# The sixth pass's finishing moves into the seventh, two normalisations to the seventh's end, and the gate turns get banks of their own: an attention megakernel on one NeuronCore

## What is computed

```python
xn = _layernorm(x, axis=-1)
s = _L0_attn_ref(xn, ...)              # gated linear recurrence, norm, silu gate, projection
g = _silu(_L0_ffn_ref(xn, ...))        # 8 experts, top 2, gates = softmax of the two logits
x = x + s * g
xn = _layernorm(x, axis=-1)            # "second normalisation" below
s = _L1_attn_ref(xn, ...)              # windowed attention
g = _silu(_L1_ffn_ref(xn, ...))        # ternary feed-forward
x = x + s * g
```

## Time and profile before

| | |
|---|---|
| median of three runs | 3416.82 us (3414.13 to 3417.32) |
| the profiled execution's own time | 3419.85 us |
| its span, first to last instruction | 3418.1 us |
| PE busy | 3286.0 us, 96% |
| DVE busy | 2671.5 us, 78% |
| ACT busy | 1834.8 us, 54% |
| POOL busy | 1272.6 us, 37% |
| mean granted TensorE clock | 0.997 |
| chain that ended last, by engine | PE 71%, DVE 12%, ACT 7%, DMA 4% |
| chain, DMA `g_wide<-gate_rows` alone | 3% |

### The profile page before, as it was taken

How to read it: one execution, slowest core, us unless ns; L and a number is a source line. 1 busy time by engine, 2 the same in 40 slices (tenths; PEclk the granted TensorE clock), 3 DMA queues, 4 the chain that set the end, 5 groups by cost and what they waited for, 6 DMA issues and landing times.

```text
span 3418.1 us, 89893 instructions
## 1 busy us (share of the span) xinstructions
PE 3286.0 (96%) x35134; PEld 2274.5 (67%) x35134; DVE 2671.5 (78%) x6395; ACT 1834.8 (54%) x4088; POOL 1272.6 (37%) x1404
## 2 busy tenths in 40 slices
PE   5999999999999999999999999999999999999998
PEld 3676666766667666676766667666676666766666
DVE  6877878878788777887778777787877878878787
ACT  3364654646546465463655636456364654646546
POOL 4434244242443524425233342423434244242432
PEclk9999999999999999999999999999999999999999
DMA  4002010020100202011020110202002010020110
GB/s 116 22 22 61 23 53 19 25 58 24 52 23 25 54 24 61 15 38 40 24 64 11 54 29 21 63 12 65 18 24 60 24 52 21 22 58 24 52 23 26
DMA packets 110005, 128.56 MB, mean 38 GB/s; under 512 B 23457, under 2 KB 77329, under 8 KB 109585
## 3 DMA queue, kind: packets, MB, share of 16 engines
q1 hardware_dynamic: 104720, 121.13, 13.7%
q10 hardware_dynamic: 4864, 1.69, 0.2%
HBM read 74.01 MB, written 17.30 MB: 27 GB/s over the span
## 4 chain that ended last, share of the span: by engine, by line
PE 71%; DVE 12%; ACT 7%; DMA 4%; issue 3%; POOL 1%; SPq 0%; DVEq 0%; ACTq 0%; POOLq 0%
PE bank L1926 7%; PE bank L1549 5%; PE bank L1945 5%; PE bank L1828 5%; PE bank L1694 4%; PE bank L1863 4%; PE bank L1889 4%; PE bank L1586 3%; DMA g_wide<-gate_rows 3%; PE bank L1711 3%; PE bank L1766 3%; PE bank L1666 3%; PE bank L1651 3%; DVE am L1268 3%; PE bank L1845 2%
## 5 line engine op out<-in xcount | busy, mean ns | idle before, releaser
L901 POOL TENSOR_TENSOR qx<-qx 128x512 f32<-128x512 f32 x256 | 277.5, 1084 | 656.9 <-ACT qx L1139 655.1
L1403 DVE TENSOR_REDUCE row_max<-bank 128x4 f32<-128x384 f32 x512 | 270.8, 550 | 90.6 <-PE bank L1828 90.1
L1268 DVE TENSOR_TENSOR am<-bank,causal 128x512 f32<-128x512 f32 x512 | 327.9, 682 | 17.6 <-PE bank L1666 17.6
L1509 DVE TENSOR_TENSOR sq_lo<-qx,sq_hi 128x512 fp32r<-128x512 f32 x256 | 232.3, 907 | 125.3 <-ACT sq_hi L1127 124.1
L1945 PE MATMUL bank<-pj_t,sq_hi 128*128 128x256 f32 x1024 | 260.3, 288 | 6.2 <-DVE sq_lo L1509 5.5
L1023 ACT ACTIVATE tanh_g<-bank 128x256 f32<-128x256 f32 x128 | 49.2, 384 | 400.8 <-PE bank L1549 400.8
L1549 PE MATMUL bank<-w_vg,xt 128*128 128x512 f32 x512 | 252.3, 615 | 0.0
L1945 PE MATMUL bank<-pj_t,sq_lo 128*128 128x256 f32 x1024 | 251.0, 279 | 0.0
L1586 PE MATMUL bank<-xt,w_down 128*128 128x512 f32 x512 | 237.2, 596 | 0.0
L1139 ACT ACTIVATE qx<-bank,scale_fc 128x512 f32<-128x512 f32 x256 | 177.2, 692 | 98.5 <-PE bank L1931 96.6
L1412 DVE TENSOR_TENSOR am<-bank,row_max 128x384 f32<-128x384 f32 x384 | 212.9, 554 | 9.8
(11 more groups left out here) (278 smaller groups left out, 8523.1 us busy)
## 6 DMA issues: line engine op xcount, KB each, us to landing
g_wide<-gate_rows SPq DMA_DIRECT2D x64, 512.0 KB, 6.1
x<-in_L_attn_x SPq DMA_DIRECT2D x128, 128.0 KB, 2.3
qt<-in_L_attn_x SPq DMA_DIRECT2D x128, 128.0 KB, 2.5
out<-x SPq DMA_DIRECT2D x128, 128.0 KB, 1.7
k<-k SPq DMA_DIRECT2D x96, 128.0 KB, 2.4
xl<-xh SPq DMA_DIRECT2D x48, 128.0 KB, 2.4
xl<-xn SPq DMA_DIRECT2D x48, 128.0 KB, 2.3
xh<-xn SPq DMA_DIRECT2D x48, 128.0 KB, 2.3
```

The lines of the kernel that those rows point to most:

```text
L901: nc.gpsimd.tensor_tensor(sq[:, n % 3, :], relu[:, n % 3, :], relu[:, n % 3, :], ALU.mult)\
L1268: nc.vector.tensor_tensor(am_tiles[:, :, j], bank[3 + j][:].rearrange("p (f e t) -> p f e t", f=2, e=2), causal[:].unsqueeze(1).unsqueeze( ...
L1403: nc.vector.tensor_reduce(row_max[:, j, :], bank[1 + j][:, 0:4 * KW].rearrange("p (h k) -> p h k", k=KW), AX.X, ALU.max, negate=(j == 0)). ...
L1509: nc.vector.tensor_tensor(sq_lo[:, n % 3, :], sq[:, n % 3, :], sq_hi[:, n % 3, :].bitcast(F32), ALU.subtract)\
```

## The change

`first_queries_keys` gets a table of banks in place of 4 + n % 4; only n = 6 changes its bank by it, from 6 to 2. `experts_down` 0 to 3 moves from banks 0, 1, 2, 3 to 2, 3, 7, 6. The gates' transposes keep banks 1 and 0, which now hold nothing of this sequence's head, and no longer wait for two Relus. ACT's two copies of gate rows move ahead of the copies of queries and keys 4 and 5. On DVE the second `finish_chunk` of pass 5 is gone, `finish_chunk(4)` runs in the gap of pass 6, only two of the four `normalise2` stay in that gap, and the other two run after `project_gated(5)`, ahead of `middle_state(7)`. Waits are changed to fit.

```diff
--- before.py
+++ after.py
@@ -303,6 +303,8 @@
     pair_turn_banks = (2, 1, 3)
     turn_banks = {6: 7, 7: 0}
     gate_banks = (1, 0)
+    down_banks = (2, 3, 7, 6)
+    first_banks = {2: 6, 3: 7, 4: 4, 5: 5, 6: 2, 7: 7}
     output_banks = (1, 1, 1, 1, 1, 1, 1, 7)
     up_banks = (2, 2, 2, 2, 2, 2, 2, 5)
     qk_banks = (5, 1, 6, 0)
@@ -915,7 +917,7 @@
                     def first_queries_keys(n):
                         g, which, half = n // 4, n // 2 % 2, n % 2
                         act.wait_ge(s["qkp_ok"], at("qkp_ok", n - 1))
-                        nc.scalar.copy((kt if which else qt)[:, half, g * 512:(g + 1) * 512], bank[4 + n % 4][:])\
+                        nc.scalar.copy((kt if which else qt)[:, half, g * 512:(g + 1) * 512], bank[first_banks[n]][:])\
                           .then_inc(s["qk_ok"], 1)
 
                     for i in range(NC // 2):
@@ -938,16 +940,16 @@
                         act.wait_ge(s["hp_ok"], at("hp_ok", i + 1))
                         if i == 4:
                             act.wait_ge(s["gkl_ok"], at("gkl_ok", NC // 2))
-                        nc.scalar.activation(hidden_t[g][:, j, :], bank[5 if g else j][:], ACT.Relu, bias=b_down[:, j:j + 1])\
+                        nc.scalar.activation(hidden_t[g][:, j, :], bank[5 if g else down_banks[j]][:], ACT.Relu, bias=b_down[:, j:j + 1])\
                           .then_inc(s["hr_ok"], 1)
 
                     experts_relu(0)
                     experts_relu(1)
-                    first_queries_keys(4)
-                    first_queries_keys(5)
                     for b in range(NG):
                         act.wait_ge(s["gtp_ok"], at("gtp_ok", b + 1))
                         nc.scalar.copy(gate_rows[:, b * 512:(b + 1) * 512], bank[gate_banks[b]][32:64, :]).then_inc(s["gx_ok"], 1)
+                    first_queries_keys(4)
+                    first_queries_keys(5)
                     experts_relu(2)
                     nc.scalar.activation(warm[:], gdiff[:, 0:1], ACT.Exp)
                     experts_relu(3)
@@ -1316,11 +1318,11 @@
                             gated_output(c - 1)
                         if c + 1 < NC:
                             experts_gate(c)
-                        if 2 <= c < NC - 2:
+                        if 2 <= c < NC - 1:
                             finish_chunk(c - 2)
                         if c == NC - 2:
                             dve.wait_ge(s["rs2"], at("rs2", 1))
-                            for b in range(4):
+                            for b in range(2):
                                 normalise2(b)
                         if c + 1 < NC:
 
@@ -1351,8 +1353,9 @@
                         if c + 1 < NC:
                             if c:
                                 project_gated(c - 1)
-                            if c == NC - 3:
-                                finish_chunk(c - 1)
+                            if c == NC - 2:
+                                for b in range(2, 4):
+                                    normalise2(b)
                             middle_state(c + 1)
                             if c < NC - 2:
                                 normalise_output(c)
@@ -1564,26 +1567,20 @@
                             if copy:
                                 pe.wait_ge(s["hqk_ok"], at("hqk_ok"))
                         elif n >= 6:
-                            pe.wait_ge(s["qk_ok"], at("qk_ok", n - 5))
+                            pe.wait_ge(s["hr_ok"], at("hr_ok", 1 if n == 6 else 3))
                         w = w_k if which else w_q
                         for k in range(KD):
-                            mm = nc.tensor.matmul(bank[4 + n % 4][:], w[:, k, half * P:(half + 1) * P],
+                            mm = nc.tensor.matmul(bank[first_banks[n]][:], w[:, k, half * P:(half + 1) * P],
                                                   xt[:, k, g * 512:(g + 1) * 512], start=(k == 0), stop=(k == KD - 1))
                         mm.then_inc(s["qkp_ok"], 1)
 
                     def experts_down(i):
 
                         g, j = i // 4, i % 4
-                        if i == 0:
-                            pass
-                            if copy:
-                                pe.wait_ge(s["lg_ok"], at("lg_ok"))
-                        elif i == 1:
-                            pass
-                            if copy:
-                                pe.wait_ge(s["hqk_ok"], at("hqk_ok"))
+                        if i in (2, 3):
+                            pe.wait_ge(s["qk_ok"], at("qk_ok", 4 - i))
                         for k in range(KD):
-                            mm = nc.tensor.matmul(bank[5 if g else j][:], w_down[:, k, j * P:(j + 1) * P],
+                            mm = nc.tensor.matmul(bank[5 if g else down_banks[j]][:], w_down[:, k, j * P:(j + 1) * P],
                                                   xt[:, k, g * 512:(g + 1) * 512], start=(k == 0), stop=(k == KD - 1))
                         mm.then_inc(s["hp_ok"], 1)
 
@@ -1594,7 +1591,8 @@
                     first_queries_keys(4)
                     first_queries_keys(5)
                     pe.wait_ge(s["gates_ok"], at("gates_ok", 7))
-                    pe.wait_ge(s["hr_ok"], at("hr_ok", 2))
+                    if copy:
+                        pe.wait_ge(s["lg_ok"], at("lg_ok"))
                     for b in range(NG):
                         for j in range(4):
                             mm = nc.tensor.transpose(bank[gate_banks[b]][:, j * P:(j + 1) * P], gates[:, 4 * b + j, :], ident[:])
@@ -1609,7 +1607,7 @@
                             pe.wait_ge(s["gkd_ok"], at("gkd_ok", 32 * (c // 2)))
                         if c == 0:
                             pe.wait_ge(s["qk_ok"], at("qk_ok", 3))
-                            pe.wait_ge(s["hr_ok"], at("hr_ok", 4))
+                            pe.wait_ge(s["hr_ok"], at("hr_ok", 2))
                         else:
                             pe.wait_ge(s["am_ok"], at("am_ok", 4 * c - 2))
                         first, second = gk_first[:, c, :], gk_second[:, c, :]
@@ -1658,6 +1656,7 @@
                         pe.wait_ge(s["dst_ok"], at("dst_ok", c + 1))
                         if c == 0:
                             pe.wait_ge(s["qk_ok"], at("qk_ok", 5))
+                            pe.wait_ge(s["hr_ok"], at("hr_ok", 4))
                         elif c <= 4:
                             pe.wait_ge(s["hr_ok"], at("hr_ok", 4 + c))
                         for half in range(2):
```

## The result

The changed kernel takes 3444.74 us, median of five runs (3435.69 to 3446.01), against 3416.82 (3413.83 to 3421.83) before: a ratio of 1.0078, 95% interval 1.0065 to 1.0091. It is slower by 27.9 us, where the forecast had 5.8: 1.7 us a sequence in place of 0.36. The profiled execution has a time of 3446.01 and a span of 3444.3; its mean granted clock is 0.990, against 0.997 before; in the other four executions the clock is 0.991 to 0.994. One of ten executions of a later variant (all four normalisations in the gap) took 4569.43 us at a mean granted clock of 0.655, is left out of its median, and the trace shown for that variant is from another execution.

What follows compares the result with a forecast made beforehand. PE is busy 96% of the span, so only its idle time could be won. DVE's moves cost 8.2 us, the earlier write gains 2.4: +5.8 us, median from 3416.8 to 3422.6, range 3411 to 3430.

Steps and rivals of the forecast that it cites:

- Part 1, what goes and what is late next: Gates' transposes lose their 1.38 us wait; the stall at `experts_up(0)` grows to 2.1 to 2.4 us a sequence.
- the 0.15 a sequence from the earlier write: SP's earlier gate-row write shortens the wait at `experts_up(0)` by 0.15 us a sequence, 2.4 us in all.
- The write gives all it can: Rival: landing of the gate rows follows issue, gaining 0.45 us in 15 sequences, 6.8 us; 3418.2 us; chance 0.14.
- Part 2: DVE, passes 5 to 7: PE's second pair of transposes in pass 7 comes 0.51 us later a sequence, costing 8.2 us.
- DVE's add is not held: Rival: in pass 6 POOL's product falls elsewhere, DVE's chain is up to 0.75 us shorter; 3410.6 us; chance 0.10.
- POOL holds the moved normalisations: Rival: POOL's `o_rstd` product lengthens the two normalisations before pass 7 by 0.6 us a sequence; 3432.2 us; chance 0.10.
- Both stalls really go: Rival: stalls at the gates and in pass 6 vanish, 2.2 us a sequence, 35 us; 3381.5 us; chance 0.07.
- The sum: Whole kernel: 8.2 - 2.4 = +5.8 us, 0.36 us a sequence, median 3422.6 us; chance 0.56.
- Slower: the clock: Rival: the longer stall before `experts_up(0)` halves PE's clock, losing 2.2 us 16 times; 3457 us; chance 0.03.

Runs made afterwards that it cites:

- all four normalisations in the gap: Kernel before with `finish_chunk(4)` moved into pass 6 and all four normalisations left in that pass's gap: 3426.05 us, ratio 1.0023.
- part 1 alone: Kernel before with the change's edits outside DVE's list (banks and order of the gate turns): 3430.67 us, ratio 1.0039.
- part 2 alone: Kernel before with only DVE's edits (`finish_chunk(4)` and two normalisations moved), head as before: 3425.05 us, ratio 1.0024.
- the stall filled: Changed kernel with 16 identity transposes, results never read, on PE before `experts_up(0)`: 3425.98 us, ratio to before 1.0027.
- six fillers: Changed kernel with six identity transposes, results never read, on PE before `experts_up(0)`: 3434.6 us, ratio to before 1.0048.
- the round trip first: Kernel before with the gates' edits, and SP writing gate rows and issuing the first half's wide reads before loading x: 3394.28 us, ratio 0.9937.
- the last look at the four normalisations: Kernel before with `finish_chunk(4)` in pass 6 and all four normalisations in its gap, run once more for its trace: 3421.84 us.

## Why the prediction was wrong

**Part 1, what goes and what is late next: right on the sum of the stalls.** The wait for the Relus was only the first of two waits on one slow chain. All of it came back at `experts_up(0)`, and the idle time of the two places stayed where it was (34.4, then 33.7 alone and 36.9 with part 2). The stall was forecast at 2.1 to 2.4 us a sequence, and 36.9 / 16 is 2.3. But the forecast took one length for all, and they ran up to 4.49.

**Part 1, the 0.15 a sequence from the earlier write: too high, by little.** The write did come 0.05 us behind the loads, but its landing did not come earlier: 2.27 us from the end of the loads' issue to the wide reads, against 2.13. On average over the second to sixteenth sequence it is 2.28 with part 1 alone and 2.29 before: nothing won. With nothing ahead of it the round trip takes 1.48. "The write gives all it can" is out. The Trainium skill, page "DMA: Bandwidth & Descriptors", section "Queues, rings and completion order", lets a transfer signal only after every earlier write of the same DMA engine; by that rule the gain is nothing, and 2.22 against 1.48 us agrees with it.

**Part 2: right, to 0.04 us.** Forecast 0.51 us a sequence; 0.53 by the trace, 0.55 by DVE's part alone. Its steps stand in the rows of the changed kernel too: 1.33 from the moments to `normalise_output`, 4.25 to the add (4.24), 1.17 for the held add, and 8.18 from the moments to `state_sum` (8.20). "DVE's add is not held" fell with the 1.17. "POOL holds the moved normalisations" fell too: the two take 0.73 us (568.05 to 568.78), as two did unheld (0.74 in the earlier trace rows), and POOL's product on one element a partition runs across them from 568.18 to 568.89. "Both stalls really go" fell with both new waits.

**The sum: wrong, by the clock.** The step that failed is the rival "Slower: the clock", which the sum put at nothing: its mechanism and its place were right, its chance of 0.03 was far too low. It set the new stall between 1.4 us, which costs nothing, and 5 us, which does, and then treated the whole gap as safe, without a row for it. The trace of before had two more rows: in its prologue PE also stood idle for 4.54 and 4.25 us, and both times the clock fell too. That narrows the gap at its upper end only; for 2.25 us no row of before spoke either way, so a price of this size belonged in the range. Its size was off in the other direction: 2.2 us in each of 16 sequences, where 11 had a fall and each cost 1.7. In place of nothing the clock took 18.8 us. The measured loss of 27.9 us is put together from 9.7 that remain with the stall filled and 18.8 that go with it (28.5; the two jobs' medians of before differ by 0.5).

**What stays open.** Alone the parts cost 14.4 and 8.8 us, 23.2, and together 27.9. The rest, 4.7, fits the falls, 8 in the trace of part 1 and 11 with both, but each is the count of one execution, and whether both parts together always have more isn't settled. Nor is which stall falls. Over six traces (the changed kernel, part 1 alone, part 2 alone, six fillers, the round trip first, and the last look at the four normalisations) no stall before `experts_up(0)` up to 1.85 us was followed by a fall, and of 34 from 1.86 to 4.5 us 24 were; one of 2.94 was not, and two of 1.86 were. Why the changed kernel's trace has a stall as long as 4.49 us isn't shown beyond its late wide reads.

## What to carry to other kernels

Before a wait is taken away, ask what chain its releaser belongs to, and whether the engine meets the same chain again a little later; then the idle time only moves, and two short stalls that become one long one can cost TensorE's clock besides. Before a block is moved on a busy engine, ask what wait it covered where it stood, and beside what it will run. Make room and fill it in one edit (`experts_down(4)` in the stall turned part 1's +14.4 us into -27.6), and put a small transfer on which a chain depends ahead of bulk loads. Look at the granted clock around each new stall, and at a busy time that grew with the same instruction count.

## What the runs showed of the hardware

A pause of PE of 1.86 to 4.5 us in a stream that is otherwise full was followed in 24 of 34 cases by 3.4 us, sometimes 6.8, at 1.2 GHz; the trace of before had it only in the prologue, after pauses of 4.25 to 5.0 us, and in its last 5 us. Small transposes that compute nothing kept the clock at 2.4 GHz in 16 of 16 sequences. Beside a 128x512 product of POOL, DVE's 128x256 add took 1.17 us in place of 0.42, where POOL's product on one element a partition left the two normalisations at 0.73. The Trainium skill, page "SBUF — State Buffer", section "Who interferes with whom", describes DVE's and GpSimd's shared ports as an exclusive lock; the 1.17 us agrees with it.
